# Weights of a group's first half built a turn ahead, the second half's between two accumulations; the gathers' lead set to 192

## What is computed

```python
e = leaky_relu(a_s[:, src] + a_d[:, dst], 0.2)
gw = softmax(gate_weights)
def head_step(acc, xs):
    h_h, e_h, g_h = xs
    m = segment_max(e_h, dst, num_segments=N)
    ex = exp(e_h - m[dst])
    den = segment_sum(ex, dst, num_segments=N)
    alpha = ex / den[dst]
    out = segment_sum(h_h[src] * alpha[:, None], dst, num_segments=N)
    return (acc + g_h * out, None)
```

## Time and profile before

| | us |
|---|---|
| median of 3 runs | 1458.57 |
| the runs | 1458.08 to 1460.7 |
| the profiled execution | 1464.55 |
| its span, first to last instruction | 1462.8 |
| PE busy | 1172.9 (80%) |
| DVE busy | 996.3 (68%) |
| POOL busy | 695.6 (48%) |
| ScalarE busy | 498.8 (34%) |

### The profile page before, as it was taken

How to read it: one execution, slowest core, us unless ns; L and a number is a source line. 1 busy time by engine, 2 the same in 40 slices (tenths; PEclk the granted TensorE clock), 3 DMA queues, 4 the chain that set the end, 5 groups by cost and what they waited for, 6 DMA issues and landing times. The chain is left out here.

```text
span 1462.8 us, 30254 instructions
## 1 busy us (share of the span) xinstructions
PE 1172.9 (80%) x6192; PEld 945.0 (65%) x6193; DVE 996.3 (68%) x2854; ACT 498.8 (34%) x1969; POOL 695.6 (48%) x782
## 2 busy tenths in 40 slices
PE   4996699999999987887661999999971799999800
PEld 4664466666666665665441888888861699999700
DVE  6565388888888888776663689989954334444378
ACT  2553233333333332222204555555520232333201
POOL 1001767666676666766501567766652011111175
PEclk9998599999999999787775999999985899999955
DMA  6162688878888887877668334334314962222156
GB/s 198 36 105 78 143 246 243 267 232 263 248 267 250 249 248 235 243 225 222 187 153 268 131 112 137 136 129 135 127 55 161 343 230 68 72 69 71 59 173 179
DMA packets 219210, 255.68 MB, mean 175 GB/s; under 512 B 57205, under 2 KB 193016, under 8 KB 215640
## 3 DMA queue, kind: packets, MB, share of 16 engines
q1 hardware_dynamic: 177464, 140.79, 30.6%
q0 software_dynamic: 30992, 103.79, 24.7%
q10 hardware_dynamic: 10640, 9.86, 2.2%
HBM read 139.69 MB, written 114.67 MB: 174 GB/s over the span
## 5 line engine op out<-in xcount | busy, mean ns | idle before, releaser
L740 POOL DMA_INDIRECT rows<-node_rows,srcT x391 | 392.9, 1005 | 182.8 <-issue 81.4
L1053 PE MATMUL pO<-rows,pw 128*128 x1184 | 338.7, 417 | 33.6 <-DVE pw L820 29.4
L836 DVE SCALAR_TENSOR_TENSOR acc<-acc,rsc,pO 128x257 f32<-128x257 f32 x592 | 281.0, 475 | 61.4 <-PE pO L1053 29.6
L1053 PEld LDWEIGHTS pO<-rows,pw 128*128 128x128 f32 x1184 | 216.3, 202 | 80.4 <-issue 52.8
L1413 PE MATMUL pW_<-W_again,aT 128*128 128x256 f32 x800 | 181.8, 381 | 1.2 <-DVE res L1481 1.1
L1413 PEld LDWEIGHTS pW_<-W_again,aT 128*128 128x128 f32 x800 | 148.6, 191 | 20.3 <-DVE res L1481 1.9
L1859 POOL DMA_DIRECT2D ys_rows<-ye x64 | 34.5, 539 | 238.8 <-DVE ye L1810 234.7
L1749 ACT ACTIVATE hT<-pHe,b 128x128 f32<-128x128 f32 x256 | 73.0, 368 | 193.6 <-PE pHe L1775 191.0
L1775 PEld LDWEIGHTS pHe<-xeT,w1e 128*128 128x128 f32 x1024 | 127.5, 196 | 13.1 <-DVE w1e L1800 9.9
L1775 PE MATMUL pHe<-xeT,w1e 128*128 128x128 f32 x1024 | 128.2, 280 | 9.2 <-DVE xeT L1793 9.2
L1784 PE MATMUL pYe<-w,hT 128*128 x512 | 121.5, 380 | 2.1 <-issue 1.3
(11 more groups left out here) (332 smaller groups left out, 1929.2 us busy)
## 6 DMA issues: line engine op xcount, KB each, us to landing
agg_rows<-acc SPq DMA_DIRECT2D x296, 256.0 KB
w<-in_ffn_w SPq DMA_DIRECT2D x32, 512.0 KB, 5.8
xe<-xs_rows ACTq DMA_DIRECT2D x64, 128.0 KB, 2.0
ys_rows<-ye POOLq DMA_DIRECT2D x64, 128.0 KB, 2.0
rows<-node_rows,srcT POOLq DMA_INDIRECT x391
node_rows<-xna SPq DMA_DIRECT2D x25, 136.0 KB, 1.8
xna<-in_x SPq DMA_DIRECT2D x5, 640.0 KB, 11.3
mix_rows<-hx SPq DMA_DIRECT2D x25, 128.0 KB
```

The costliest lines, as they stand in the source:

```text
L740: pool.indirect_dma_start(rows[:, k % RING, :], None, node_rows[:, :], at_row(srcT[:, k:k + 1])).then_inc(s_rows[k % len(s_rows)], 16)
L836: dve.scalar_tensor_tensor(out=acc[:, k % VA, s % HG, 0:D + 1], in0=before, scalar=rsc[:, g % V2, s:s + 1], in1=pO[n % PB][:, 0:D + 1], op ...
L1053: pe.matmul(pO[n % PB][:, 0:D + 1], pw[:, s // HG, s % HG, :], rows[:, ds(at[s % 4], 1), 0:D + 1].rearrange("p c f -> p (c f)"), start=Tru ...
```

## The change

Two things. LEAD goes from 96 to 192. On DVE, `spread(0)` moves from the head of the turn with lag 2 to the tail of the turn before with lag 1, between accumulations 13 and 14 (so it builds the first half for the group that follows), and `spread(1)` moves, with lag 2 as before, behind `leaky` and `max_upto` of the next group, between accumulations 1 and 2. The waits within the stages, PE's, ScalarE's, POOL's and SP's orders are the same.

```diff
--- before.py
+++ after.py
@@ -38,7 +38,7 @@
 ONE, AS = D, D + 1
 RW = 272
 DST_PAD = 4080
-RING, FLY, LEAD, AHEAD = 55, 4, 96, 2
+RING, FLY, LEAD, AHEAD = 55, 4, 192, 2
 PARTS = 4
 HP = HG // PARTS
 TAB = 20
@@ -889,9 +889,9 @@
                                                     rz[:, QH + g * 4:QH + g * 4 + 4].unsqueeze(2).to_broadcast([P, 4, HD]), ALU.mult)
                         ins.then_inc(on_sb.sem, 1)
 
-                    groups([(2, spread(0)), (2, spread(1)), add[0], add[1], (1, leaky), (1, max_upto), add[2], add[3], (1, max_chain), (1, max_after), add[4], add[5],
+                    groups([add[0], add[1], (1, leaky), (1, max_upto), (2, spread(1)), add[2], add[3], (1, max_chain), (1, max_after), add[4], add[5],
                             (1, max_carry), add[6], (1, max_top), (1, max_less), add[7], (0, z_sum), (0, mask_eq), (0, bias_parts), (0, z_inverse), add[8], (0, divide), (0, mask_ad), add[9], (1, old_scale), add[10],
-                            (1, old_keep), add[11], (1, clear_ml), (1, top_lasts), *add[12:14], (2, resets), (2, heads), *add[14:]])
+                            (1, old_keep), add[11], (1, clear_ml), (1, top_lasts), *add[12:14], (1, spread(0)), (2, resets), (2, heads), *add[14:]])
 
                     wait(dve, md_ps, 0)
                     for j in range(2):
```

## The result

| | before | after |
|---|---|---|
| median, us | 1458.32 (4 runs) | 1470.88 (4 runs) |
| the runs, us | 1457.54 to 1460.7 | 1466.52 to 1473.51 |
| ratio | | 1.0079, 95% interval 1.0051 to 1.0108 |
| profiled execution, us | 1464.55 | 1466.52 |
| its span, us | 1462.8 | 1464.7 |

By the medians the change costs 12.6 us, by the ratio 0.8%, with an interval of about 7 to 16 us; the forecast was 7.9. The sign and the first links held. The sizes, and the share of each link in the loss, did not all hold.

A forecast was written before the change was run, and what follows sets the result against it. POOL's gathers up to group 35, then two turns and a half turn of DVE and PE, were taken to bound the end. Held gathers +10 us and tail -2.1 on 1458.6 gave 1466.5 us, range 1455.5 to 1476.

The forecast's parts named there:

- The lead: POOL's limit on gathers: raising LEAD from 96 to 192 does neither good nor harm, no time.
- The deciding term: POOL's gathers: builds set apart each hold their own gather, 20 us over 35 turns, half taken as passing through, +10 us.
- the ring: Buffer of gathered chunks: might start to bind, consumers up to 18 us later mid-stage; part of a rival with chance 0.14.
- Alone, these edits would leave the end of the gathers where it is: Changed turn lengths: consumers 14 us later at group 32 but level by group 35, so POOL's end stays.
- Turns with a tile: 22 turns where PE also does a node tile: each about 0.85 us longer, 18 to 19 us in all.
- Groups 32 to 35: Three late turns, waiting for POOL before: about 15.6 us each in place of 20.8, if POOL allows.
- Turns without a tile: 8 turns where PE waits for the builds: net gain 0.5 us each, 4 us in all.
- the tail: Turns behind group 35, no longer waiting for POOL: 17.02 becomes about 15.9 us, last half turn gains 1.0, together -2.1.
- (a): Rival at POOL: its waits absorb the holds, no change, 1456.5 to 1459 us; chance 0.22.
- (b): Rival, faster: holds absorbed, the ends of the turns decide, about 1455 us; chance 0.14.
- (d): Rival at PE: extra pause lowers its clock in node-tile turns, 1 to 2 us each, up to 1490 us; chance 0.04.
- (c): Rival: all held gather time passes through, +20 - 2.1, 1476.5 us, or the ring starts to bind; chance 0.14.

The follow-up runs named there:

- first_only: Kernel before with only the first half's build moved, to the tail of the turn before; 1468.87 us, ratio 1.0078.
- pb3_before: Kernel before with products in three PSUM banks in place of four, pexp still in SBUF; 1459.84 us, ratio 1.0012.
- psum_before: Kernel before with three product banks and pexp in the fourth PSUM bank; 1453.15 us, ratio 0.994.
- moves_only: Kernel before with both builds moved as in the change, LEAD left at 96; 1469.02 us, ratio 1.0084.
- psum_after: Changed kernel with three product banks and pexp in the fourth PSUM bank; 1469.43 us, ratio 1.006.
- psum_first: first_only with three product banks and pexp in the fourth PSUM bank; 1452.18 us, ratio 0.9941, in a second batch 1453.07 us, 0.9941.
- lead_only: Kernel before with LEAD set to 192, DVE's order as before; 1458.04 us, ratio 1.0001.
- ring44_before: Kernel before with a ring of 44 slots in place of 55; 1464.4 us, ratio 1.0022.

## Why the prediction was right or wrong

**The times together.** Ratios to the kernel before:

| order of builds | `pexp` in SBUF | `pexp` in PSUM, nothing held |
|---|---|---|
| before | 1 | 0.994 |
| first half a turn ahead only | 1.0078 | 0.9941 |
| as changed | 1.0079 | 1.006 |

Freeing the gathers gains 0.6% in the first line, 1.4% in the second and at most a little in the third. Read the other way: without holds, building the second half in the middle costs 1.2%; with holds it costs nothing on top of them. The two costs of the change do not add. Against the kernels that have neither (0.994), the holds alone cost 1.4% (1.0078 / 0.9941), the middle alone 1.2% (1.006 / 0.9941), and both together 1.4% (1.0079 / 0.9941). That they don't add, to 2.6%, is clear of the intervals, each about 0.4% wide to a side; that the later of the two gives the end is how I read it, by the waits of ScalarE at group 35.

**The lead: right.** No time, alone (1.0001) or beside the moves (1.0084 without it, 1.0079 with it).

**The deciding term: right as a mechanism, not the only one.** Builds set apart hold a gather each, and that alone costs about what I put on it: in `first_only` 21.5 us are held and 9.0 lengthen POOL's stretch, and from `pb3_before` to `psum_before` 15.7 us of holds go and 8.1 us of stretch (571.1 to 563.0). So about the half that I took as the middle of two bounds came out; no row had pointed to it. The size was off in the changed order itself: forecast a mean of 1055 ns, measured 1026 and, in `moves_only`, 1047. Why these differ is open. It is not the ring, which delays POOL by some 5 us in both.

The Trainium skill (SBUF — State Buffer, section "SBUF: two separate sides") has a VectorE instruction with two SBUF inputs shut out a GpSimd one that reads SBUF. The trace agrees from both sides: gathers that begin under a build take up to 2.00 us with two, 0.95 with one in PSUM. The same sentence lets whichever starts first block the other; of that only one direction is seen here, as the last section tells.

**The step that failed** is the cost of the longer turns, in the sentence "Alone, these edits would leave the end of the gathers where it is". `psum_after` is that case, with no holds: its stretch is 575.2 us against 568.4 and 561.8 of `psum_first`, 7 to 13 us more. Three terms were undersized:

- Turns with a tile: +0.85 forecast, +1.00 measured, 22 us in 22 turns and not 18 to 19. The build passed on its full 1.14 us to `max_chain`; small waits took back 0.08 and not 0.15, and the boundary gave 0.05 and not 0.13, because I looked at product 0 there and not at the scores behind it, which wait for ScalarE.
- Groups 32 to 35: 15.6 forecast, 16.52 measured. In after, the scores at 689.08 us took 0.77 us (row below) against 0.46 in the earlier trace rows, and the granted clock was 0.91 from 680 to 720: PE's clock still falls to 1.2 GHz in some of these turns. I had carried a turn at the upper clock through to the end. Three turns make 2.8 us. (In `moves_only` they take 17.5 us, but there the last one waits for POOL.)
- The ring. I set it into a rival with 0.14, as a by-case of "everything passes through". The queue stands at it in every profile of this order, for 16 to 31 gathers, and POOL is delayed by 5 us (after and `moves_only`) to 14 (`psum_after`). In the trace of before, those gathers had 12 to 18 us to spare, against 22 us by which the 22 turns grow. That comparison was there to be made, and I made it only for the lead's side.

```profile
689.08 0.77 PE L1004 MATMUL pM<-cst,asb 128*128 128x128 f32 x2 [1.37 <-ACT asb L922]
```

So the consumers were not level with before at group 35 but 5.9 us later (`leaky` 35 less `leaky` 2: 525.6 against 519.7 us), and POOL's stretch is 7.3 us longer: its gathers take 8.3 us more, and its idle time is 1.0 less. In `first_only`, with the ring out of reach, 12.7 us of the idle time were used up. That the forecast came near was in part luck: in that trace the holds added 8 us and not 20, and the longer turns, put at nothing, added their part.

**Turns without a tile and the tail: right in this pair of traces, not shown for the order.** -0.42 a turn (forecast 0.5), 15.91 at group 35 to 36 (forecast 15.9), and from `leaky` 35 to the last accumulation 40.8 us against 42.8 (forecast -2.1). But the four other profiles with DVE's order of before (`lead_only`, `pb3_before`, `psum_before`, `ring44_before`) have 15.11 to 16.44 us for the first, 15.04 to 17.13 for the second and 39.2 to 43.3 for the third. That spread is larger than the gain, so part of the agreement is luck. PE's waits for `pw` of 2.25 us are gone; what ends the turn is ScalarE, as the working had it:

```profile
607.29 1.13 PE L1053 MATMUL pO<-rows,pw 128*128 x4 [0.92 <-DVE acc L836]
609.75 0.46 PE L1004 MATMUL pM<-cst,asb 128*128 128x128 f32 x2 [1.32 <-ACT asb L922]
```

**The rivals.** (a) and (b) needed the holds to be absorbed; `first_only` shows that two fifths of them pass through, and `psum_before` about half. (d) did not happen: from 200 to 520 us the granted clock stays at 1.00. (c) was right that the ring starts to bind, not that everything passes through.

**What stays open.** How many of the 12.6 us are due to holds and how many to turns in the changed kernel itself can't be said, as the two lie over each other: in one profile both arrive together at group 35, in another of the same order POOL is 3.7 us later. What the ring costs at its 55 slots is not shown either, as no run made it longer; the shorter rings show only that POOL's head start counts in this order. And `psum_after` pays something for its third bank: turns without a tile take 16.04 us against 15.69, with PE's idle time before products at 63.5 us in place of 22.9. That is some 3 us in 8 turns, and no run has the changed order with three banks and `pexp` in SBUF. Turns with a tile are no longer than in after (15.92 against 15.93), so most of the 1.2% should stand.

**A faster kernel.** `pexp` in PSUM, with the order of before or with the first half a turn ahead, is 0.6% faster than before, in three comparisons. The two orders don't differ measurably.

## What to carry to other kernels

Where two engines run side by side with a buffer of limited depth between them, lay the growth of the consumer's turns beside the producer's slack at the buffer, in microseconds, before calling an edit in the consumer free. Two delays that end at the same join don't add: an experiment that removes one can show nothing although that one alone would cost as much, so test each without the other. And where an instruction with two SBUF inputs holds gathers, look for an input that can live in PSUM before moving the instruction about.

## What was not expected of the hardware

A build of 1.2 us with one of its inputs in PSUM takes as long as with both in SBUF (1209 to 1218 against 1210 to 1220 ns), and a gather that begins under it takes 0.95 us in place of up to 2.00 (66 such gathers in before, 63 in `psum_first`, where none takes longer than 0.95); the largest of 391 gathers was 1195 ns in `psum_before`, 1997 before. The hold goes one way only, in these traces. In before, 55 builds begin while a gather is running: they take 1.22 to 1.25 us, as the others do, and the median of those gathers is 0.95. Timelines of DVE and of POOL in before, a pair of builds that begins under a running gather:

```profile
193.69 2.35 DVE L820 TENSOR_TENSOR pw<-pexp,eq 128x1024 f32<-128x1024 f32 x2
```

```profile
193.00 0.95 POOL L740 DMA_INDIRECT rows<-node_rows,srcT  x1 [0.30 <-PE pO L1053]
194.25 1.48 POOL L740 DMA_INDIRECT rows<-node_rows,srcT  x1 [0.30 <-issue]
```

The pair of builds takes its usual 2.35 us and the gather that was already running its usual 0.95. Only the next one, begun under a build, is held.

With the same builds in the same order, the gathers' mean still moved between 992 and 1005 ns from one execution to another. And the changed kernel is slower at a higher clock, 0.915 against 0.892: before, PE stood more often (9.64 us for group 35 on ScalarE's side, 2.25 us for `pw`), and a fuller PE had the higher clock without an earlier end.
